# Four reorderings in a float32 expert tower: softmax between the mixing operations, strip-wise shared units, a halved first unit, and the output product in four column groups

## The reference

```
eo = relu(einsum('bed,edh->beh', xe, W) + b)            # 10 experts, each 1024 x 1024
gates = softmax(einsum('btd,tdk->btk', x[:, :T], Gw) + Gb)
task_out = einsum('btk,btkh->bth', gates, eo[:, SEL])   # own 2 experts and the 2 shared ones
gs = softmax(x[:, T] @ Gsw + Gsb)                       # layer 0 only
shared_out = einsum('be,beh->bh', gs, eo)               # over all 10 experts
h = relu(concat(z, dense_ctx) @ W_top1 + b_top1)        # 4112 -> 512
y = relu(h @ W_top2 + b_top2) @ W_top3                  # 512 -> 256 -> 1
```

## Time and profile before

| what | us |
|---|---|
| median of 3 runs | 2011.32 (2009.89 to 2011.5) |
| profiled execution, its own time | 2009.13 |
| its span, first to last instruction | 2007.1 |
| PE busy | 1981.2 |
| DVE busy | 1382.6 |
| ACT busy | 706.4 |
| PE idle until the first gathered rows | 8.1 |
| PE idle for `w_lo` | 11.6 |
| PE idle for `act_lo` at a change of step | 2.8 |

### The profile page before, as it was taken

The page is one execution under the profiler, slowest core; times in us unless marked ns, Lnnn a source line. Parts: engine busy times, 40 slices in busy tenths (PEclk is TensorE's granted clock), DMA queues, the critical chain, the costliest instruction groups (busy, mean ns, idle before and its releaser), DMA issues.

```text
span 2007.1 us, 25673 instructions
## 1 busy us (share of the span) xinstructions
PE 1981.2 (99%) x8848; PEld 1606.6 (80%) x8848; DVE 1382.6 (69%) x1447; ACT 706.4 (35%) x944; POOL 168.6 (8%) x152
## 2 busy tenths in 40 slices
PE   8999999999999999999999999999999999999999
PEld 6878778787878787878878778787878778878787
DVE  4488988896256766667555888898953667666664
ACT  3233232323333333332434333323233233423333
POOL 4630000000030002122033000000000000000000
PEclk9999999999999999999999999999999999999999
DMA  6553324243353334343344424234333433333331
GB/s 214 173 161 108 125 84 134 87 130 99 95 158 95 118 94 150 105 140 115 100 146 135 129 84 139 89 124 129 94 98 95 118 96 117 95 118 94 116 94 43
DMA packets 70017, 232.69 MB, mean 116 GB/s; under 512 B 10094, under 2 KB 12654, under 8 KB 69948
## 3 DMA queue, kind: packets, MB, share of 16 engines
q1 hardware_dynamic: 61688, 210.76, 34.7%
q0 software_dynamic: 7488, 20.98, 3.2%
q10 hardware_dynamic: 772, 0.10, 0.0%
HBM read 231.58 MB, written 0.23 MB: 115 GB/s over the span
## 4 chain that ended last, share of the span: by engine, by line
PE 93%; DVE 3%; issue 2%; ACT 1%; DMA 0%; SPq 0%; ACTq 0%; DVEq 0%
PE main L334 28%; PE main L336 28%; PE main L335 28%; PE top L334 3%; PE top L335 3%; PE top L336 3%; PE gps L374 1%; DVE prod L878 1%; DVE w_lo L804 1%; DVE eo_b L878 1%; ACT w_hi L500 0%; DVE act_lo L816 0%; DVE slots L884 0%; DMA raw<-in_w_first 0%; ACT eo_b L504 0%
## 5 line engine op out<-in xcount | busy, mean ns | idle before, releaser
L334 PE MATMUL main<-act_hi,w_hi 128*128 128x512 f32 x2568 | 1002.8, 390 | 15.2 <-DVE w_lo L804 11.6
L335 PE MATMUL main<-act_lo,w_hi 128*128 128x512 f32 x2568 | 999.6, 389 | 0.0
L336 PE MATMUL main<-act_hi,w_lo 128*128 128x512 f32 x2568 | 999.2, 389 | 0.0
L804 DVE TENSOR_TENSOR w_lo<-raw,w_hi 128x1024 fp32r<-128x1024 f32 (+1 forms) x356 | 433.3, 1217 | 566.4 <-ACT w_hi L500 534.8
L500 ACT ACTIVATE w_hi<-raw 128x1024 fp32r<-128x1024 f32 (+1 forms) x356 | 375.8, 1056 | 1172.3 <-PE main L336 1058.3
L334 PEld LDWEIGHTS main<-act_hi,w_hi 128*128 128x128 f32 x2568 | 481.9, 188 | 136.2 <-issue 31.0
L336 PEld LDWEIGHTS main<-act_hi,w_lo 128*128 128x128 f32 x2568 | 482.0, 188 | 100.8
L335 PEld LDWEIGHTS main<-act_lo,w_hi 128*128 128x128 f32 x2568 | 482.0, 188 | 99.2
L884 DVE TENSOR_TENSOR slots<-slots,prod 128x1024 f32<-128x1024 f32 (+2 forms) x202 | 245.1, 1213 | 6.0
L325 POOL DMA_INDIRECT slots<-in_tbl,idx x144 | 164.5, 1143 | 910.4 <-DVE act_lo L816 613.0
L878 DVE TENSOR_TENSOR prod<-eo_sh,gate_b 128x1024 f32<-128x1024 f32 x136 | 165.7, 1218 | 2.3 <-DVE slots L884 0.5
(11 more groups left out here) (65 smaller groups left out, 455.4 us busy)
## 6 DMA issues: line engine op xcount, KB each, us to landing
raw<-in_w SPq DMA_DIRECT2D x304, 512.0 KB
gate_b<-gates_dram SPq DMA_DIRECT2D x34, 512.0 KB
raw<-in_w_top SPq DMA_DIRECT2D x32, 512.0 KB
raw<-in_w_first SPq DMA_DIRECT2D x16, 512.0 KB
gate_b<-gates_dram SPq DMA_DIRECT2D x16, 256.0 KB
slots<-in_tbl,idx POOLq DMA_INDIRECT x144
gw<-in_g_w SPq DMA_DIRECT2D x16, 128.0 KB
raw<-in_w_top SPq DMA_DIRECT2D x4, 256.0 KB
```

What stands on the lines that cost most here:

```text
L334: nc.tensor.matmul(dst, lhs_hi, rhs_hi, start=start, stop=False)
L335: nc.tensor.matmul(dst, lhs_hi, rhs_lo, start=False, stop=False)
L336: return nc.tensor.matmul(dst, lhs_lo, rhs_hi, start=False, stop=stop)
L804: nc.vector.tensor_tensor(w_lo[0:parts, slot, 0:cols], raw[0:parts, rawslot, 0:cols], w_hi[0:parts, slot, 0:cols], ALU.subtract).then_inc( ...
```

## The change

1. `WARM`: 18 transposes of the identity are put ahead of the gathered rows on PE.
2. Unit 0 of the program is done in two column halves of 256. Two k-strips share a bank, so ACT and DVE take two 256-column pieces at once, the first four pairs when two of the four gathered blocks are turned. Two k-strips of the first half are multiplied before the last block is transposed, the others after it. Unit 0 then has 48 matmuls of 256 columns instead of 24 of 512.
3. Softmax: on DVE `shifted` now stands ahead of the `w_lo` split of the step's third unit, and `gate_rows` behind it. In layer 0 the last two mixing operations of a change (`keep=2`) move behind `gate_rows`. The in-place transposes of gathered rows that stood in units 1 and 2 of two tasks move to units 2 and 3.
4. Shared experts of layer 1: PE runs the first two units interleaved, six k-strips of the first, three of the second, the last two of the first, the last five of the second (`first_two`). ACT splits the second unit's weights ahead of activation strips 6 and 7, and DVE in the middle of the last pair's mixing.
5. `tower3` runs as four column groups of 128 columns each, in four groups of partitions; ACT copies 128 x 128, and the DMA takes four rows of 128.

```diff
-        x0_bank = [main[0], gps[0], main[1], gps[1]] + top
+        x0_bank = [main[0], gps[1]] + top + [gps[0], main[1]]
...
+            def first_two(U, E, S):
+                pe.wait_ge(evac_done, E - 1)
+                pe.wait_ge(hi_split, U + 1)
+                pe.wait_ge(lo_split, U + 1)
+                strips(0, U, range(0, 6), S)
+                pe.wait_ge(evac_done, E)
+                pe.wait_ge(hi_split, U + 2)
+                pe.wait_ge(lo_split, U + 2)
+                strips(1, U + 1, range(0, 3))
+                strips(0, U, (6, 7), S)
+                strips(1, U + 1, range(3, KT))
...
-                    mm = nc.tensor.matmul(bank[0:1, :], w3[:, k:k + 1], eo_b[:, k, :],
-                                          start=(k == 0), stop=(k == MT2 - 1))
+                    for c in range(QUADS):
+                        n = slice(c * Y_COLS, (c + 1) * Y_COLS)
+                        mm = nc.tensor.matmul(bank[c * QUAD:c * QUAD + 1, 0:Y_COLS], w3[:, k:k + 1], eo_b[:, k, n],
+                                              start=(k == 0), stop=(k == MT2 - 1))
...
+            for n in range(WARM):
+                nc.tensor.transpose(gps[0][:, 0:P], ident, ident)
...
+            for bt in range(X0_HALF + 1):
+                x0_turn(bt)
+            pe.wait_ge(hi_split, 1)
+            pe.wait_ge(lo_split, 1)
+            x0_sums(0, range(2))
+            x0_turn(X0_HALF + 1)
+            x0_sums(0, range(2, KT))
+            x0_sums(1, range(KT)).then_inc(unit_done, 1)
+            logits(0, from_halves)
```

ACT, in `change`:

```diff
                 evacuate(main[1][:, :], dest(STEP - 1), bias(STEP - 1))
+                split_hi(1, (off + 1) % RAW, V + (off + 1) // RAW)
                 if shared:
                     act.wait_ge(sh_done, shared + 3)
                     hand_over(S, chunk, (6,), U)
-                split_hi(1, (off + 1) % RAW, V + (off + 1) // RAW)
```

DVE, in `step` and then in `change`:

```diff
                 for j in range(1, STEP - 1):
+                    if j == 1 and gates:
+                        shifted(*gates)
                     split_lo(U + j + 1, (j + 1) % 2, (off + j + 1) % RAW, V + (off + j + 1) // RAW)
                     if j == 1 and gates:
-                        shifted(*gates)
                         gate_rows(*gates)
-                    if j == 2:
+                    if j == (1 if gates else 2):
                         run(late)
...
                     hand_over(S, chunk, range(0, 6))
                     run(b3[:2])
-                    hand_over(S, chunk, (6,))
+                    split_lo(U + 1, 1, off + 1, V)
                     run(b3[2:4])
-                    hand_over(S, chunk, (7,))
-                    split_lo(U + 1, 1, off + 1, V)
+                    hand_over(S, chunk, (6, 7))
...
-                run(b2 + b3)
+                rest = b2 + b3
+                run(rest[:len(rest) - keep])
+                return rest[len(rest) - keep:]
```

## The result

The changed kernel takes 1999.44 us (median of 6 runs, 1999.08 to 1999.94) against 2010.61 for the kernel before (6 runs, 2009.04 to 2011.83): a ratio of 0.9946, 95% interval 0.9936 to 0.9957. I had predicted 2001.0, in a range of 1996.5 to 2005.5. The profiled execution took 1999.35 us.

The account below looks back on a forecast made before the run. PE bounds the kernel, busy 1981.2 of 2007.1 us, so time is its work plus gaps. Terms 1.0 + 1.9 + 4.3 + 1.1 + 2.0 = 10.3 us, from 2011.32 to 2001.0; range 1996.5 to 2005.5.

Parts of the forecast that it names:

- Softmax: DVE's order in layer-0 tasks: six third-unit gaps 0.16 us shorter each, 1.0 us; one fourth-unit gap of 1.9 us gone.
- The 0.16 us: Added to each PE gap's bracketed wait, because the next product would start 0.23 us later but the record before lasts 0.39.
- The covers of the fourth units and of layer 1: Weight splits ready before PE needs them: by 0.5 us in layer-0 fourth units, 0.6 in layer 1's second task.
- Rival A: The six third-unit gaps in layer-0 tasks go altogether, giving another 9 us: 1992; chance 0.08.
- Strips: Shared experts of layer 1: interleaving the first two units saves 2.15 us, twice, 4.3 in all.
- Start: Program start: the halved unit 0 ends at 19.1 us instead of 20.17, 1.1 us gained.
- The product of 256 columns at 0.12: Halved unit 0 on PE: each product of 256 columns takes 0.12 us, near the transposes' 0.11.
- Output product: Output product in four column groups: 1.0 us gained in the first half; 0.75 plus 0.3 for ACT's copy at the end; 2.0.
- rival D: PE stays at its lower clock longer from the start: gain gone over 20.6 us, 30 us give 2016; chance 0.04.

Follow-up runs that it names:

- the experiment with four kept: Changed kernel with four mixing operations instead of two kept for behind the softmax in layer 0, two transposes moved to the second task's last units: 1989.45 us, ratio 0.9896.

## Why the prediction was right

The time was 1.6 us under the forecast. The sum of 10.3 stands against 9.7 in the profiles and 11.2 in the medians (2010.61 less 1999.44), and the forecast added it to 2011.32, the median of three runs; six runs gave 2010.61, and beside the experiments the kernel before took 2009.6 to 2009.9. So 0.7 us of the miss is in that base. From the profiled execution the same sum gave 1998.8, and 1999.35 was measured.

- *Softmax*, 1.0 + 1.9: measured 0.8 + 1.95, and 2.91 when undone. The exchange of two mixing operations for `shifted` is nearly even, as the rows had it. The 0.16 us that the prediction adds to each bracket is too little: the first product behind a gap also takes 0.31 us to its successor instead of 0.23, so that it is 0.24. The covers of the fourth units and of layer 1 held. Rival A was wrong in its mechanism, but the 9 us that it put on those gaps were there: the experiment with four kept took them.
- *Strips*, 4.3: measured 4.3 in the profiles, 4.4 in the medians when done alone in the kernel before, and 6.3 when undone. What I missed is the granted clock's drop behind this gap, and with it a part of what the change does: the kernel before scatters over 2.8 us, the changed one over 0.9.
- *Start*, 1.1: 0.6 between the two profiles, 2.1 in the medians when undone, and 1.0 to 1.3 for the halving alone. The product of 256 columns at 0.12 was right; the rule of the Trainium skill (TensorE: Matmul & The Clock Gate, The mechanism) that speaks against hidden loads of the same rows is again not what the trace shows, with loads of 0.19 us. Wrong was that transposes would go at 0.11: they went at 0.21 until 11.7. The profile of before had caught a good run, with the earliest rise of the clock of the five without a warm-up and the earliest rows, and I took its pace as given. That 0.6 and 2.1 lie around 1.1 is luck.
- *Output product*, 2.0: measured 1.26 + 0.58. In the middle the forecast was 1.0: eight records of 128 columns in four groups take 0.40 with the last one's end, 0.02 apart, so I was too careful. At the end PE's 0.76 and the 0.31 of ACT's copy are as forecast (0.75 and 0.3), but the sum put the DMA of four rows at nothing, and it costs 0.49. The total is near because these two errors have opposite signs.
- *Clock, rival D*: the slow pace lasted until 11.7 us, 0.4 longer than in the profile of before and far from the 20 us more that D needed. My reading of the clock column, 1.00 at 8.1 to 10.2, as 2.4 GHz was wrong: there is no record of the clock in that stretch. The drop exists elsewhere, behind the shared gap, and the change took that gap away. It did not take away every drop: single runs of the changed kernel (1999.94, the slowest of six) and of three of its variants also have a mean clock of 0.999, and no trace shows where.

## What to carry to other kernels

When PE is busy 99% of the time, list its gaps by place, and for each the queue that stands ahead of the releasing instruction on its engine; four mixing operations kept for later in the kernel before were worth as much as the whole change, 10.9 us, and putting a block of nearly equal length in the place of two of them was worth 0.8 on the same gaps. Before an instruction is moved behind a wait, look at the steps that have no gap: there it may be the one on the chain.

## What the runs showed of the hardware

A gap of 1.4 us and one of 0.2 close behind were followed at two of eight places by eight products at 0.43 instead of 0.23 us, with the granted clock at 0.66 over 5 us; the six gaps of 1.5 us in the tasks were not, in any profile here. At the start of the program transposes ran at 0.21 and later at 0.11 us, and the trace's first record of the clock, at 2.4 GHz, stood within 0.1 us of the change in 14 profiles; ahead of it the view's 1.00 was no measurement. A DMA of four rows of 512 bytes took 0.58 us to issue, one of a row of 2048 bytes 0.24. Sixteen weight loads of one column with products of 128 columns, four column groups at a time, took 0.55 us in all.
